# A layered cross-attention, ternary feed-forward and routed-expert kernel: scatters in pairs over more units, one weight split behind the last scatters, two statistics later

## The reference, cut to what matters

```python
x = x + xattn0(layernorm(x), ctx)       # scores against projected context, normed, softmax
x = x + ffn0(layernorm(x))              # Hadamard-rotated 8-bit tokens, ternary weights, 512-2048-512
x = x + xattn1(layernorm(x), ctx, ctx)  # 32 query heads, 8 key/value heads, head size 16
x = x + moe(layernorm(x))               # 8 experts, 2 per token, silu(x@w0)*(x@w1) @ wo, inner 1024
```

## Time and profile before

| what | value |
|---|---|
| median of 3 runs | 1664.45 us (1662.42, 1664.45, 1666.59) |
| profiled execution, own time | 1672.16 us |
| its span | 1670.3 us |
| mean granted PE clock | 0.975 |
| PE, DVE, ACT, POOL busy | 94%, 57%, 43%, 42% of the span |

### The profile page before, as it was taken

The page is one execution under the profiler, slowest core; times in us unless marked ns, Lnnn a source line. Parts: engine busy times, 40 slices in busy tenths (PEclk is TensorE's granted clock), DMA queues, the critical chain, the costliest instruction groups (busy, mean ns, idle before and its releaser), DMA issues.

```text
span 1670.3 us, 24439 instructions
## 1 busy us (share of the span) xinstructions
PE 1567.2 (94%) x8124; PEld 1047.5 (63%) x8150; DVE 948.0 (57%) x1539; ACT 717.6 (43%) x1160; POOL 702.1 (42%) x479
## 2 busy tenths in 40 slices
PE   6869999999889999999899899999999999999998
PEld 4555657565543434434333778788788888788886
DVE  6998979796878897887885622222122222222221
ACT  5885646455547777777677211111111111111111
POOL 1124251633513125254354765670862180930064
PEclk9889999999898999999999999999999999999999
DMA  9189800000231445243430625231440140530088
GB/s 357 56 305 386 291 1 1 0 1 1 84 94 47 123 132 149 82 126 111 148 114 28 224 70 189 82 120 32 182 176 26 59 155 26 188 127 26 26 140 213
DMA packets 90944, 196.16 MB, mean 117 GB/s; under 512 B 7153, under 2 KB 9074, under 8 KB 90226
## 3 DMA queue, kind: packets, MB, share of 16 engines
q1 hardware_dynamic: 71746, 156.68, 28.2%
q0 software_dynamic: 7168, 17.04, 4.5%
q10 hardware_dynamic: 11952, 21.43, 3.9%
HBM read 113.28 MB, written 81.32 MB: 117 GB/s over the span
## 4 chain that ended last, share of the span: by engine, by line
PE 68%; DVE 16%; POOL 6%; ACT 4%; issue 3%; DMA 3%; another core or an unknown queue 0%; SPq 0%; POOLq 0%; DVEq 0%; ACTq 0%
PE psum L2929 11%; PE psum L2931 11%; PE psum L2930 11%; PE psum L2580 6%; DVE neg_max L2057 5%; PE psum L2782 5%; PE psum L2771 5%; PE psum L2744 4%; POOL expert_weight_parts L1052 3%; PE psum L2625 3%; PE psum L2595 2%; DMA w_of_even_expert<-in_L_ffn_w 2%; PE psum L2953 2%; POOL expert_weight_parts L1051 1%; DVE inner_rotated_t_second L1926 1%
## 5 line engine op out<-in xcount | busy, mean ns | idle before, releaser
L2057 DVE TENSOR_REDUCE neg_max<-psum 128x2 f32<-128x1024 f32 x248 | 291.3, 1220 | 49.5 <-PE psum L2744 48.3
L1420 ACT ACTIVATE probabilities<-psum 128x512 f32<-128x512 f32 x512 | 271.7, 601 | 85.2 <-PE psum L2771 81.3
L2199 DVE TENSOR_TENSOR expert_inner<-psum,expert_inner 128x512 f32<-128x512 f32 x78 | 53.9, 692 | 388.7 <-ACT expert_inner L1526 378.6
L2929 PE MATMUL psum<-expert_weight_parts,sorted_tokens_t_first 128*128 x624 | 250.8, 402 | 8.8 <-POOL expert_weight_parts L1052 5.1
L2930 PE MATMUL psum<-expert_weight_parts,sorted_tokens_t_first 128*128 x624 | 246.8, 396 | 0.0
L2931 PE MATMUL psum<-expert_weight_parts,sorted_tokens_t_second 128*128 x624 | 246.8, 395 | 0.0
L1526 ACT ACTIVATE expert_inner<-psum 128x512 f32<-128x512 f32 x78 | 46.7, 599 | 396.7 <-PE psum L2931 396.7
L2771 PE MATMUL psum<-query_rows,key_rows 50*128 50x512 f32 x512 | 179.3, 444 | 4.1 <-ACT probabilities L1420 3.0
L2744 PE MATMUL psum<-key_rows,query_rows 48*128 48x512 f32 x496 | 170.6, 491 | 11.7 <-DVE neg_max L2057 5.8
L2929 PEld LDWEIGHTS psum<-expert_weight_parts,sorted_tokens_t_first 128*128 128x128 f32 x624 | 117.7, 189 | 37.4 <-issue 11.1
L2782 PE MATMUL psum<-probabilities,value_and_one 128*32 128x512 f32 x1024 | 140.3, 620 | 0.8 <-ACT probabilities L1420 0.7
(11 more groups left out here) (316 smaller groups left out, 2924.3 us busy)
## 6 DMA issues: line engine op xcount, KB each, us to landing
sorted_x<-zero_rows SPq DMA_DIRECT2D x9, 3960.0 KB, 30.5
w_of_odd_expert<-in_L_ffn_w SPq DMA_DIRECT2D x8, 2048.0 KB
wo_of_expert<-in_L_ffn_wo SPq DMA_DIRECT2D x7, 2048.0 KB, 8.6
query_rows<-query_rows_of_units SPq DMA_DIRECT2D x64, 192.0 KB, 3.5
w_of_even_expert<-in_L_ffn_w SPq DMA_DIRECT2D x6, 2048.0 KB, 11.6
sorted_tokens<-sorted_x ACTq DMA_DIRECT2D x39, 264.0 KB, 2.8
sorted_y<-expert_out ACTq DMA_DIRECT2D x39, 256.0 KB
query_rows_of_units<-dims_first SPq DMA_DIRECT2D x32, 256.0 KB
```

Source lines behind the costliest of these rows:

```text
L1420: nc.scalar.activation(prob[t % 2][:, i * SEQ:(i + 1) * SEQ], bank[4 + n % 3], ACT.Exp, scale=HD ** -0.5).then_inc(c_e, 1)
L2057: nc.vector.tensor_reduce(of_pair[:, p, st, :], ring(("max", (m, i))).rearrange("p (h n) -> p h n", h=2), AX.X, ALU.max, negate=True).then ...
L2199: nc.vector.tensor_tensor(h, bank[2 * half + 1], h, ALU.mult).then_inc(e_h, 1)
L2929: nc.tensor.matmul(out_bank, hi[:, cols], w_r[:, bass.ds(w_at, 512)], start=start, stop=False)
```

## The change

`SCATTERED_AT` takes the place of the two scatter halves. Batch 0 is scattered one tile (two indirect DMAs) a unit in units 15 to 18, batch 1 one tile in units 23 and 24 and two in 25, batch 2 two tiles in units 30 and 31 as before. The pieces of w0 are loaded in units 26 and 27, in place of 25 and 26. Both halves of w1's split stand behind the last scatters. In the last chain `choose(3, 0)` and `choose(3, 1)` come ahead of the wait for the inverse root. The last batch's statistics for phase C go to the ends of units 3, 4 and 5. PE makes six unread products at the end of step 0.

```diff
@@ -501,6 +501,8 @@
 
 
         ROUTED_AT = {0: 11, 1: 19, 2: 26}
+        SCATTERED_AT = {15: (0, (0,)), 16: (0, (1,)), 17: (0, (2,)), 18: (0, (3,)), 23: (1, (0,)), 24: (1, (1,)), 25: (1, (2, 3)),
+                        30: (2, (0, 1)), 31: (2, (2, 3))}
         routing_jobs = {}
         for b_, u_ in ROUTED_AT.items():
             routing_jobs[(u_ + 1, 1)] = [("xt", (b_, 0))]
@@ -739,11 +741,11 @@
                     chunk_rows(*chunk)
                 if 4 <= u < 12:
                     first_expert(u)
-                if u in (25, 26):
+                if u in (26, 27):
                     sp.wait_ge(*scattered(0))
                     sp.wait_ge(*scattered(1))
-                    first_expert(2 * (u - 25))
-                    first_expert(2 * (u - 25) + 1)
+                    first_expert(2 * (u - 26))
+                    first_expert(2 * (u - 26) + 1)
                 if routing(u, 0) is not None:
                     keep_batch(routing(u, 0))
 
@@ -907,15 +909,12 @@
                         b = routing(u, 4)
                         slots(pool, nc.gpsimd, c, b)
                         row_weights(pool, nc.gpsimd, b)
-                        scatter(b, 0)
-                    if routing(u, 5) is not None:
-                        scatter(routing(u, 5), 1)
+                    if u in SCATTERED_AT:
+                        scatter(*SCATTERED_AT[u])
                     if u in (27, 28):
                         if u == 27:
                             w_in_ready(0)
                         half_split(w_in_raw[0][0], W_IN[0][0], u - 27, w_in_parts, u - 27)
-                    if u == UNITS - 2:
-                        half_split(w_in_raw[0][1], W_IN[0][1], 0, w_in_parts, 0)
 
             def inverse_deviation(b):
                 pool.wait_ge(r_var, b + 1)
@@ -941,15 +940,15 @@
                 rows = [xr[b][k][:].rearrange("p (t c) -> p t c", c=WIDE)[:, :, 0:D] for k in range(2)]
                 nc.gpsimd.tensor_copy(rows[1], rows[0]).then_inc(d_dup, 1)
 
-            def scatter(b, half):
-
-                if b == 0 and half == 0:
+            def scatter(b, tiles_of_batch):
+
+                if b == 0 and tiles_of_batch[0] == 0:
                     pool.wait_ge(d_zf, 16 * (ZEROED + 1))
                 pool.wait_ge(d_slot, 2 * (b + 1))
                 pool.wait_ge(d_wt, 2 * (b + 1))
                 pool.wait_ge(d_xn, ST * (b + 1))
                 pool.wait_ge(d_dup, b + 1)
-                for st in (2 * half, 2 * half + 1):
+                for st in tiles_of_batch:
                     t = b * ST + st
                     for k in range(2):
                         pool.indirect_dma_start(out=sorted_x, out_offset=bass.IndirectOffsetOnAxis(ap=slot[k][:, t:t + 1], axis=0),
@@ -1013,7 +1012,8 @@
                 pool.wait_ge(c_x, UNITS)
                 inverse_deviation(BATCH - 1)
                 last_scatters()
-                half_split(w_in_raw[0][1], W_IN[0][1], 1, w_in_parts, 1)
+                for h in range(2):
+                    half_split(w_in_raw[0][1], W_IN[0][1], h, w_in_parts, h)
                 pool.wait_ge(*scattered(2))
                 wo_split(0)
 
@@ -2079,6 +2079,10 @@
                         last_dims_out(1)
                     if (u, t) == (UNITS - 1, 3):
                         last_dims_out(2)
+                if u in (3, 4):
+                    tokens_statistics(BATCH - 1, u - 1)
+                if u == 5:
+                    queries_deviation(BATCH - 1)
                 if u == UNITS:
                     last_attended_added()
                 if u > 1 and u % KVH == 1:
@@ -2181,10 +2185,12 @@
 
             def phase_d():
                 b = BATCH - 1
+                choose(b, 0)
+                choose(b, 1)
                 dve.wait_ge(r_rstd, BATCH)
                 nc.vector.scalar_tensor_tensor(out=shift[:], in0=mv_all[:, 2 * b * ST:2 * (b + 1) * ST:2], scalar=-1.0,
                                                in1=rstd_all[:, b * ST:(b + 1) * ST], op0=ALU.mult, op1=ALU.mult).then_inc(r_var, 1)
-                for part in range(6):
+                for part in range(2, 6):
                     choose(b, part)
                 top_weight(b)
                 row_weights(dve, nc.vector, b)
@@ -2297,9 +2303,6 @@
                 dve.wait_ge(c_ones, 4)
                 nc.vector.memset(gw[:], 0.0).then_inc(c_ones, 1)
                 attention(-1)
-                tokens_statistics(BATCH - 1, 2)
-                tokens_statistics(BATCH - 1, 3)
-                queries_deviation(BATCH - 1)
                 dve.wait_ge(c_ones, 5)
                 for u in range(UNITS + 1):
                     attention(u)
@@ -2953,6 +2956,8 @@
                             last = nc.tensor.transpose(bank[5 + half][:, k * P:(k + 1) * P],
                                                        h_d[:, (4 * half + k) * P:(4 * half + k + 1) * P], ident[:])
                         last.then_inc(e_htr, 1)
+                    if static(i) and i == 0:
+                        unread(6, bank[7])
 
                 pe.wait_ge(d_plan, 1)
                 transpose_x(0, 0)
```

## The result

The change was forecast at 1661.0 us (1656 to 1667). Its median is 1669.14 us (15 runs), beside 1663.19 us for the kernel before in the same comparison: ratio 1.0031 [1.0021, 1.0040]. So it is outside the range and on the wrong side. The difference is small, but its interval leaves out no change.

What follows compares the result with a forecast made beforehand. PE was busy for 94% of the span, so only its waits or slow work could count. Terms -0.6 - 4.0 - 1.2 + 2.4 + 1.7 - 1.7 = -3.4 us, laid on the 1664.45 us median: 1661.0 us (1656.0 to 1667.0).

Steps and rivals of the forecast that it cites:

- scatter term: Phase C, units 16, 17 and 24: scatters in pairs remove PE's gaps, -4.0 us, between -8.0 and 0.
- rival B: Phase C: the gaps are not the scatters' doing, so the scatter term is 0; 1665.0 us, chance 0.17.
- Unit 25: Phase C: four scatters left in this unit bring half a chance of a gap with its clock, +1.7 us.
- the splits behind the scatters: POOL's list in phase C: 2 us later costs nothing, as SP fetches the rows a unit later.
- rival D: Phase D's start: DVE's L2242 slips behind POOL's second subtraction, w0 starts 4 us late; 1662.6 us, chance 0.03.
- Statistics: Ahead of unit 0 a gain of 1.7 us, in later units a loss of 1.1; sum -0.6 us.
- The last chain: End of phase C: root, `choose` and scatters come sooner, w0's first product at 949.2; -1.2 us, between -2.1 and 0.
- The wait for w1: Step 0 of phase D: PE waits for w1, its halves split behind the last scatters; +2.4 us.
- The clock behind it: Step 0, behind the wait for w1: the clock falls, +1.7 us, between 0 and 7.2.
- Unread products: End of step 0: six products fill PE's gap and keep the clock up; -1.7 us, between -1.8 and +0.5.
- rival C: Step 0: the new wait for w1 lowers the clock for the step's rest; price 2.4 + 7.2 us, chance 0.07.

Runs made afterwards that it cites:

- e9: The kernel before, unedited, run again beside the comparison's own: 1663.21 us, ratio 0.9995.
- e1: The kernel before with only the last batch's statistics and deviation moved to units 3, 4 and 5: 1674.15 us, 1.0010 of before.
- e3: The kernel before with only the new last chain, w1's halves behind the scatters and the unread products: 1670.88 us, 0.9991 of before.
- e14: e1 unedited, on another chip: 1675.13 us, 1.0009 of before.
- e2: The kernel before with only the spread scatters and w0's pieces in units 26 and 27: 1666.81 us, 0.9970 of before.
- e4: The changed kernel with only the statistics put back ahead of unit 0: 1666.97 us, 0.9967 of before.
- e13: The changed kernel, unedited, where before stood at 1674.12 us: 1668.34 us, 0.9963 of before.
- e15: The changed kernel with statistics behind tile 2's maxima in units 3 and 5, deviation in unit 7: 1667.91 us, 0.9971 of before.
- e16: e4 with w1's first half back in unit 30 and batch 1's last pair of scatters behind unit 26's split: 1665.18 us, 0.9949 of before.
- e11: e3 unedited, on another chip: 1665.73 us, 1.0011 of before.
- e10: e2 unedited, on another chip: 1666.97 us, 1.0015 of before.
- e12: e4 unedited, on another chip: 1665.27 us, 1.0007 of before.
- e6: e4 with w1's first half split in unit 29, behind a wait for the logits: 1673.54 us, 1.0059 of before.
- e17: The changed kernel with two filler products behind each maximum ahead of unit 0: 1666.39 us, 1.0014 of before.
- e5: The changed kernel, unedited, where before stood at 1663.85 us: 1668.71 us, 1.0028 of before.

## Why the prediction was wrong

**The step that failed is the scatter term, and ahead of it the sentence "I work out a difference against it and lay that on the median".** Of the profile's excess over the median, 7.7 us, the gaps' 8.0 us were about the whole. A median that low had no gaps in it: in e9, the same program, units 16, 17 and 24 take 36.58 us and not 44.40. I saw this (rival B, "the gaps may belong to profiling", 1665.0 us, chance 0.17), and gave the nearness of the scatters more weight. Both were true: the gaps are the scatters' doing where they occur (with the scatters as before e1, e3 and e14 have them, spread over more units e2, e4, e13, e15 and e16 on the same two chips have none), and they don't occur on every chip (e9, e11). Measured alone, the term is -5.0 us where before stands at 1672 (e2) and +2.5 where it stands at 1665 (e10), against my -4.0. The forecast was -3.4 us and the change costs 5.0 (1.0030). By e10 alone the scatter term is 6.5 of these 8.4 us. By e12, where scatters and chain together cost 1.2 us against a forecast -2.8, it is 4.0 with the chain, and 4.4 fall on the statistics.

**Unit 25.** I put +1.7 us on half a chance of a gap of the kind in the earlier trace rows. None of that kind came, but PE's wait there grew all the same: 0.7 us by POOL's split over DVE's operation, and in most profiles 1.1 more in unit 26 by the clock behind it. That the sum is near 1.7 is luck. I had written that 2 us cost nothing to the splits behind the scatters, since rows are fetched a unit later. The cover held for the rows. What it left out is whom the split itself holds once it runs later. That is rival D's mechanism at another place, DVE held until POOL's subtraction ends: L2137 (0.17 to 0.85 us), L2153 in e6 (0.19 to 4.06) and L2248 after the change (4.13, as in the earlier trace rows). The Trainium skill, "SBUF — State Buffer", section "SBUF: two separate sides", says that of a GpSimd operation and a VectorE one that needs the ports which the two share, the one that starts first gets them for its whole instruction. The trace agrees in these three places.

**Statistics.** The gain of 1.36 us and the loss of 1.3 are near the terms (1.7 and 1.1). Not in the sum was the clock of unit 0: 3.1 us where it comes back late. The whole change less its pieces without statistics is 1.0030 - 1.0007 on chips without gaps, 3.8 us. Alone the statistics cost 1.5 to 1.7 us (e14, e1), with intervals that include no change. On chips with gaps the whole change (e13, 0.9963) and the same without statistics (e4, 0.9967) are alike by their ratios, 1.4 us apart by their medians. So the statistics cost between nothing and 3.8 us. That the late clock is this cost is likely (e15, e17), not proven: e5's profile, of the unedited change, has no late clock (unit 0 lasts 12.23 us), and its median is 1668.71 all the same.

**The last chain.** In the whole change the mechanics were as forecast. The root starts 0.1 us behind its input and no more behind scatters, `choose` starts ahead of the shift (though behind the root, which ends at 919.33), and w0's first product comes 53.57 us behind the last copy of maxima instead of 54.92 (1.35 us; forecast 1.2). **The wait for w1** is 2.16 us, and step 0's products take 2.43 us longer by it (forecast 2.4). **The clock behind it** stayed at 1.00, so +1.7 was 0: a wait of PE does not always bring the clock down. **Unread products**: the gap went from 1.48 to 0.20 us and no slow stretch followed; from the transposes of step 0 to those of step 1 it is 15.03 us instead of 16.56, so -1.5 (forecast -1.7). In the profiles these three come to -0.45 us.

Alone, the part measures -1.5 us (e3, an interval that includes no change) and +1.8 (e11, one that leaves it out). Their profiles show where the gain of the chain went: w0's first product comes 55.04 and 55.00 us behind the last copy, as in before. In both, the clock is at its lower level for some 3.5 us as the chain begins. PE's windows of e11:

```profile
905.00:910.00 5.00, 3.59 (x22) 0.84 0.53 211
910.00:915.00 5.00, 4.95 (x28) 0.82 0.58 215
```

The logits then come 1.5 us later behind the last copy than in e12. e9, the kernel before, has the stretch too, so I can't charge it to the edit; other dips, of 1.4 to 1.7 us each, sit at other places in each profile.

**A slip in rival C**: it says "slower than before from a scatter term of -2 on". By its own price the sum is +2.1 with a term of -4.0, so it is slower from -6.1 on, and by 0.3% from -1.1 on.

**What stays open**: why some chips have the gaps, what ACT and DVE wait for in them, and what brings the clock back at 510 to 512 us or only at 517 to 519. Also open is what it was in the spread that took the gaps away: fewer scatters in a row, or what else runs beside them, since the fours of units 15 and 25 show no gap on the same chips. No run differed in the chip alone for the whole set. e10's +2.5 us is near what its profile shows, 1.8 in units 25 and 26 and 0.2 to 0.7 ahead of w0's first product, but its interval reaches from 0.7 to 4.2.

## What to carry to other kernels

When the profiled execution is longer than the median by about the price of what you mean to remove, the median may not hold it: get a second profile before forecasting. Before moving POOL work later, list the DVE operations that it will then lie over, not only those that read its result. And compare a small change on several chips: here the sign went with the chip, since the changed kernel stood at 1668 to 1669 us everywhere and the kernel before at 1663 to 1665 or at 1672 to 1674.

## What was not expected of the hardware

Beside groups of four indirect DMAs, ACT, DVE and with them PE stood for about 2 us (2.27 and 1.68 in e14 for ACT and DVE), on some chips and not on others. At the end of unit 16 all four profiles of before's scatters on such chips have it, in unit 24 two of the four. And a higher granted clock is not always time: e17 won back 7 us of clock for 2.5 us. Part of it lies ahead of unit 0, where DVE's maxima set the pace at either level: eight take 9.15 us in e12 at the lower level, ten take 11.41 in e17 at the upper one, 1.14 us each. In unit 0 it is time: 12.13 us in e17 and 15.70 in e13, where PE is busy throughout.
